# Attention scores from two float32r parts on half the array's rows in place of three bfloat16 parts

## The reference

```python
def _attn(q_in, k_in, v_in, wq, bq, wk, bk, wv, bv, wo, bo, causal):
    Q = (q_in @ wq + bq).reshape(Bq, Sq, H, HD)          # H, HD = 16, 16
    Kp = (k_in @ wk + bk).reshape(Bq, Sk, H, HD)
    V = (v_in @ wv + bv).reshape(Bq, Sk, H, HD)
    scores = jnp.einsum('bqhd,bkhd->bhqk', Q, Kp) / jnp.sqrt(jnp.float32(HD))
    if causal:
        scores = jnp.where(mask, scores, -jnp.inf)
    a = jax.nn.softmax(scores, axis=-1)
    o = jnp.einsum('bhqk,bkhd->bqhd', a, V).reshape(Bq, Sq, Dm)
    return o @ wo + bo
...
x = _layernorm(x + _attn(x, x, x, ..., True), ln1_g, ln1_b)
x = _layernorm(x + _attn(x, encoder_output, encoder_output, ..., False), ln2_g, ln2_b)
x = _layernorm(x + _moe(x, router_w, router_b, e_w1, e_b1, e_w2, e_b2), ln3_g, ln3_b)
```

## Time and profile before

| | |
|---|---|
| time, median of 3 runs | 755.05 us (754.03 to 757.26) |
| span of the profiled execution | 755.9 us |
| PE busy | 711.2 us, 94% |
| DVE busy | 499.0 us, 66% |
| ACT busy | 369.2 us, 49% |
| POOL busy | 287.3 us, 38% |
| mean DMA rate | 186 GB/s |

### The profile page before, as it was taken

One profiled execution on the slowest core, in us unless ns is written; L12 is line 12 of the kernel. 1 busy time (PEld: TensorE's weight loads), 2 busy tenths in 40 slices (PEclk: granted clock), 3 DMA queues, 4 the chain that ended last, 5 costly groups with the idle time before them and its releaser, 6 DMA issues.

```text
span 755.9 us, 14560 instructions
## 1 busy us (share of the span) xinstructions
PE 711.2 (94%) x4969; PEld 478.4 (63%) x4969; DVE 499.0 (66%) x1376; ACT 369.2 (49%) x749; POOL 287.3 (38%) x558
## 2 busy tenths in 40 slices
PE   6889999999999999999997889999999999999983
PEld 4444434545464454645563666898999999999941
DVE  5679788678766877756687744365666665666436
ACT  4325475665666676677753436433433332332403
POOL 8305521542653463624654333212332332232114
PEclk9999999999999999999997989999999999999997
DMA  8954431343164021316037762676999999999754
GB/s 273 291 145 128 114 98 46 84 129 128 34 179 127 13 60 48 92 43 179 14 113 237 223 210 95 204 262 226 357 328 343 343 326 341 343 332 333 236 187 163
DMA packets 95154, 140.29 MB, mean 186 GB/s; under 512 B 11855, under 2 KB 81077, under 8 KB 92597
## 3 DMA queue, kind: packets, MB, share of 16 engines
q1 hardware_dynamic: 76357, 107.86, 45.5%
q10 hardware_dynamic: 15072, 22.02, 9.1%
q0 software_dynamic: 3648, 9.45, 3.5%
HBM read 110.65 MB, written 28.65 MB: 184 GB/s over the span
## 4 chain that ended last, share of the span: by engine, by line
PE 75%; issue 8%; DVE 7%; DMA 5%; POOL 2%; ACT 1%; SPq 0%; DVEq 0%; ACTq 0%; POOLq 0%
PE out_acc L984 11%; PE score_pair L961 10%; PE work L932 9%; PE score_pair L855 8%; PE work L849 8%; PE work L906 6%; PE work L855 4%; PE score_pair L849 3%; PE work L1008 3%; DVE neg_part_max L1472 3%; PE work L918 2%; PE work L992 2%; PE work L935 2%; DMA arena<-parts_scratch 1%; PE out_acc L849 1%
## 5 line engine op out<-in xcount | busy, mean ns | idle before, releaser
L1472 DVE TENSOR_REDUCE neg_part_max<-work 128x1 f32<-128x512 f32 (+4 forms) x368 | 213.3, 625 | 70.4 <-PE work L935 35.9
L1244 ACT ACTIVATE arena<-score_pair 128x1024 f32<-128x1024 f32 (+2 forms) x224 | 178.9, 839 | 79.8 <-PE score_pair L961 78.9
L932 PE MATMUL work<-arena 96*128 96x77 bf16 (+4 forms) x640 | 118.5, 278 | 10.3 <-ACT arena L1207 2.7
L961 PE MATMUL score_pair<-arena 99*128 99x512 bf16 (+2 forms) x448 | 104.2, 337 | 4.0 <-DMA arena<-negmax_scratch 3.0
L984 PE MATMUL out_acc<-arena 128*32 128x512 f32 (+4 forms) x896 | 103.7, 517 | 2.6 <-DVE arena L1492 2.6
L1904 POOL DMA_INDIRECT chosen_scratch<-arena,scatter_rows x36 | 35.6, 989 | 176.5 <-DVE arena L1404 176.2
L855 PE MATMUL score_pair<-arena 128*128 128x256 f32 x432 | 97.6, 380 | 0.0
L932 PEld LDWEIGHTS work<-arena 96*128 96x128 bf16 x640 | 49.5, 99 | 74.5 <-issue 31.0
L1960 POOL TENSOR_SCALAR_AFFINE_SELECT arena<-arena 128x256 f32<-128x256 f32 x128 | 51.5, 410 | 117.9 <-ACT arena L1244 116.7
L1177 ACT ACTIVATE arena<-work,expert_b_cols 128x128 f32<-128x128 f32 x180 | 51.1, 369 | 77.3 <-PE work L849 64.0
L849 PE MATMUL work<-arena 128*128 128x128 f32 x720 | 87.7, 279 | 0.3 <-issue 0.3
(11 more groups left out here) (257 smaller groups left out, 955.0 us busy)
## 6 DMA issues: line engine op xcount, KB each, us to landing
arena<-in_L_xattn_e_w SPq DMA_DIRECT2D x54, 1024.0 KB, 7.1
arena<-parts_scratch SPq DMA_DIRECT2D x24, 768.0 KB, 6.1
arena<-in_L_xattn_e_w ACTq DMA_DIRECT2D x18, 1024.0 KB, 6.4
parts_scratch<-arena_more SPq DMA_DIRECT2D x24, 384.0 KB, 2.6
parts_scratch<-arena_more SPq DMA_DIRECT2D x24, 256.0 KB, 3.0
parts_scratch<-arena_more SPq DMA_DIRECT2D x24, 128.0 KB, 2.9
residual<-in_x SPq DMA_DIRECT2D x4, 512.0 KB, 8.1
tokens_scratch<-residual SPq DMA_DIRECT2D x2, 1024.0 KB, 5.4
```

The source lines that it names most:

```text
L932: m = pe.matmul(bank[:, j * it.w:(j + 1) * it.w], qa[st.half(it.g)][0:R_S, h, n0:n0 + P], k, start=True, stop=not it.last)
L961: m = pe.matmul(st2[pair][0:rows, j, 0:w], k, qa[st.half(it.g)][0:R_M, h, skip:QG], start=True, stop=True)
L1244: act_e.activation(pt[buf][0:rows, :, 0:w], st2[pair][0:rows, :, 0:w], ACT.Exp, scale=float(HD) ** -0.5).then_inc(pair_taken[pair], 1)
L1472: dve.tensor_reduce(pm[:, it.at, it.t, it.h0:it.h0 + it.nh], bank[:, 0:it.nh * it.w].rearrange("p (j k) -> p j k", j=it.nh), AX.X, ALU.max ...
```

## The change

Queries and keys are split into two float32r parts in place of three bfloat16 parts. float32r is float32 in memory; the first part is what is left when a float32 is written as float32r, the second the rest. There are then 3 groups (part pairings 0-0, 0-1, 1-0), so that a head takes 48 rows (`R_S`) and with two parts of the maximum 50 (`R_M`). Two heads, an even and an odd one, stand one above the other: in rows 0 to 49 and 64 to 113 (`ROWS` = 64). The key and query tiles hold `HALF` = 4 columns of heads of 4 bytes in place of 8 of 2 bytes.

A maximum's bank now holds heads of one half only (`pair`), and the pieces alternate between the halves. The mask is added from the same half, in two turns of 64 rows of the identity; the lower and the upper half of the mask are also kept exchanged in `mask_qk[:, 1]`, written by two small DMAs. A turn covers all heads of the bank. The cross keys are 78 wide (`SEW`), one column of it filler. The two matmuls of a score pair go to different halves, and each raises `pair_full`. `rest` becomes one subtraction on POOL, and for the stages in a hurry is gone from ACT and DVE. Maxima are split in two, transposed by one float32 matmul. ACT waits for `prob_taken` by name before it writes `pt`. The keys' and queries' tiles move to memory of their own, which the experts' weight rings use later. `ORDER` is new.

```diff
-Q_PART = (0, 0, 0, 1, 1, 2)
-K_PART = (0, 1, 2, 0, 1, 0)
+Q_PART = (0, 0, 1)
+K_PART = (0, 1, 0)
...
-R_M = R_S + 3
+R_M = R_S + 2
+ROWS = P // 2
+HALF = HH // 2
+SEW = SE + SE % 2
...
-            steps += [Item("max", st=st, t=qb, g=u, at=c, w=w, h0=h0, nh=BANK // w, last=(c + 1) * BANK >= keys)
-                      for h0 in range(0, HH, BANK // w)]
+            steps += [Item("max", st=st, t=qb, g=u, at=c, w=w, h0=h0, nh=BANK // w, last=(c + 1) * BANK >= keys, pair=j)
+                      for h0 in range(0, HALF, BANK // w) for j in range(2)]
...
-    "mwuqm2qmwm2q2m3wmgq2m3wqmqm2f2wmqfqm3wymqsfqm3wmf2wm2q2pm2qf2wuqm2vm2q2m2rf3wmq2lm2fwqm2f2wfqfqm3gqf2wqmdumf"
+    "wmq2dyfsumfwqm3qwm3fq2mwfqfmfmqmwqrmfdqrf2m2qmlwm2wqm3q2mwfm2wfqm2qmqpfmquwqm2vmqmwmqm2wmqmfqdmqwpfm2fqwmqgmfmufpf"
...
-                    for j in range(it.nh):
-                        h = it.h0 + j
-                        k = kac[st.slot][0:R_S, h, 0:it.w] if st.cross else ka[st.slot][0:R_S, it.at, h, 0:it.w]
-                        m = pe.matmul(bank[:, j * it.w:(j + 1) * it.w], qa[st.half(it.g)][0:R_S, h, n0:n0 + P], k,
-                                      start=True, stop=not it.last)
-                        if it.last:
-                            m = pe.matmul(bank[:, (j + 1) * it.w - P:(j + 1) * it.w], identb[:, :], mask_qk[:, :],
-                                          start=False, stop=True)
+                    half = it.pair * ROWS
+                    rows = slice(half, half + R_S)
+                    for i in range(it.nh):
+                        h = it.h0 + i
+                        k = kac[st.slot][rows, h, 0:it.w] if st.cross else ka[st.slot][rows, it.at, h, 0:it.w]
+                        m = pe.matmul(bank[:, i * it.w:(i + 1) * it.w], qa[st.half(it.g)][rows, h, n0:n0 + P].bitcast(f32r),
+                                      k.bitcast(f32r), start=(i == 0), stop=(i == it.nh - 1 and not it.last))
+                    rows = slice(half, half + ROWS)
+                    for turn in range(2 if it.last else 0):
+                        to = bank[:, 0:it.nh * it.w].rearrange("p (h k) -> p h k", h=it.nh)[:, :, it.w - P:it.w]
+                        mask = mask_qk[rows, turn, :].rearrange("p (o k) -> p o k", o=1)
+                        m = pe.matmul(to, identb[rows, turn * ROWS:turn * ROWS + P], bc(mask, [ROWS, it.nh, P]),
+                                      start=False, stop=(turn == 1))
...
-                    for t in range(QT):
-                        m = pe.transpose(rows[:, t * P:(t + 1) * P],
-                                         negp[:, it.g * QT + t, :, :].rearrange("p k h -> p (k h)"), identb[:, :])
-                    m.then_inc(full[it.bank], 1)
+                    pe.transpose(bank[0:2 * HH * QT, 0:P], negp[:, it.g].rearrange("p j k h t -> p (j k h t)"),
+                                 ident[:, :]).then_inc(full[it.bank], 1)
...
-                        h = it.quad * QUAD + it.pair * 2 + j
+                        h, part = it.quad * 2 + it.pair, slice(j * ROWS, j * ROWS + R_M)
...
-                        m = pe.matmul(st2[pair][0:rows, j, 0:w], k, qa[st.half(it.g)][0:R_M, h, skip:QG],
-                                      start=True, stop=True)
-                    m.then_inc(pair_full[pair], 1)
+                        m = pe.matmul(st2[pair][0:rows, j, 0:w], k.bitcast(f32r),
+                                      qa[st.half(it.g)][part, h, skip:QG].bitcast(f32r), start=True, stop=True)
+                        m.then_inc(pair_full[pair], 1)
...
-                    e.wait_ge(pair_full[pair], it.n // 2 + 1)
-
+                    e.wait_ge(pair_full[pair], 2 * (it.n // 2 + 1))
+
+                    e.wait_ge(prob_taken[buf], it.n // 4)
...
-                    own.inc(pool.tensor_tensor(f, f, p[0], ALU.subtract))
-                    e.wait_ge(gstep, own.n)
-                    own.inc(pool.tensor_copy(p[1], f))
-                    e.wait_ge(gstep, own.n)
-                    pool.tensor_tensor(p[2], f, p[1], ALU.subtract).then_inc(third_g, 1)
+                    pool.tensor_tensor(p[1], p[1], p[0], ALU.subtract).then_inc(second_g, 1)
...
-                        sp.dma_start(to.rearrange("p h t -> p (h t)"),
-                                     parts_d[st.n, at, it.g].rearrange("g (d h) t -> (g d) (h t)", h=HH)).then_inc(
-                            qk_in[st.half(it.g)], 16)
+                        for j in range(2):
+                            rows = slice(j * ROWS, j * ROWS + R_S)
+                            sp.dma_start(ka[st.slot][rows, it.g] if at else qa[st.half(it.g)][rows],
+                                         apart(parts_d[st.n, at, it.g], j)).then_inc(qk_in[st.half(it.g)], 16)
```

More of the change, by code:

```diff
@@ L39 @@
 R_S = NGR * HD
-R_M = R_S + 3
-TWO_ONES = float(np.array([0x3F803F80], np.uint32).view(np.float32)[0])
+R_M = R_S + 2
+ROWS = P // 2
+HALF = HH // 2
+SEW = SE + SE % 2
 NEG = -1e30
@@ L168, in maxima @@
         if st.cross:
-            steps += [Item("max", st=st, t=qb, g=u, w=SE, h0=h0, nh=HH // 2) for h0 in range(0, HH, HH // 2)]
+            steps += [Item("max", st=st, t=qb, g=u, w=SEW, nh=HALF, pair=j) for j in range(2)]
             continue
@@ L373, in build @@
 def build(nc, x, ctx_in, par, wts, router_w, w1, b1, w2, b2, out):
[L374 removed]
+    f32, f32r, bf16, i32, u32 = (mybir.dt.float32, mybir.dt.float32r, mybir.dt.bfloat16, mybir.dt.int32,
+                                 mybir.dt.uint32)
     ALU, ACT, AX = mybir.AluOpType, mybir.ActivationFunctionType, mybir.AxisListType
@@ L460, in build @@
         b1_rows = onat_words[1][0:E * FC, D:D + P]
-        part_words = cut("more", 3 * S)
-        part_sb = [part_words[:, a * 3 * S // 2:(a + 1) * 3 * S // 2].bitcast(bf16).rearrange("p (k t) -> p k t", k=3)
-                   for a in range(2)]
-        mT = cut_bf("more", QG)
+        part_words = cut("more", 4 * S)
+        part_sb = [part_words[:, a * 2 * S:(a + 1) * 2 * S].rearrange("p (k t) -> p k t", k=2) for a in range(2)]
+        mT = cut("more", P)
         rT = [cut("more", D).rearrange("p (c n) -> p c n", c=KC) for _ in range(2)]
@@ L546, in build @@
         n_used = sb("tiles_used", [1, 1], i32)
+        with nc.sbuf_tensor("keys_queries", [P, KEYS], f32) as keys_t:
+            keys = keys_t[:, :]
+            ka = [keys[:, a * HALF * S:(a + 1) * HALF * S].rearrange("p (u h t) -> p u h t", u=NG, h=HALF) for a in range(2)]
+            k0 = 2 * HALF * S
+            qa = [keys[:, k0 + a * HALF * QG:k0 + (a + 1) * HALF * QG].rearrange("p (h t) -> p h t", h=HALF)
+                  for a in range(2 * NG)]
+            k0 += 2 * NG * HALF * QG
+            kac_words = keys[:, k0:KEYS]
+            kac = [kac_words[:, a * HALF * 80:(a + 1) * HALF * 80].rearrange("p (h t) -> p h t", h=HALF) for a in range(2)]
+        late = sb("weights_results", [P, KEYS])
+        w1_ring = [late[:, a * EW:(a + 1) * EW].rearrange("p (c f) -> p c f", c=KC) for a in range(RING1)]
+        w2_ring.insert(0, late[:, RING1 * EW:(RING1 + 1) * EW].rearrange("p (c n) -> p c n", c=FC))
+        assert (RING1 + 1) * EW <= 2 * HALF * S and len(w2_ring) == RING2
+        chosen = late[:, 2 * HALF * S:2 * HALF * S + 2 * NT * D].rearrange("p (c t n) -> p c t n", c=2, t=NT)
         st2 = [stack.enter_context(nc.psum_tensor(f"score_pair{i}", [P, 2, BANK], f32)) for i in range(2)]
```

186 lines of the change are left out of this document (83 added, 103 removed).

## The result

The changed kernel takes 832.09 us (median of 4 runs, 830.09 to 852.29), the kernel before 754.99 us beside it: ratio 1.1005, 95% interval 1.0966 to 1.1045. One of the four executions (852.29 us) is a slow one, which ratios leave out, and where the profiled execution of an experiment was such a one (e5, e6, e7, e13), the others' clock is given beside it. The profiled execution spans 828.5 us, 72.6 more than before. The forecast of 741 us was wrong, in its direction too, and the time lies 7 us above the range.

A forecast was written before the change was run, and what follows sets the result against it. TensorE (PE) was taken to bound attention, so PE work was summed: scores -38.1, maxima -18, masks +13.9, loads +19, shape changes +12.5, transposes -1.8, start -2, giving -14.5 from 755: 741 us, range 716 to 825.

The forecast's parts named there:

- Price of a column, 0.42 ns: Score matmuls: a float32r column was taken to stream in 0.42 ns, as in bf16; bounds 0.42 and 1.69.
- Halves side by side: Scores: the two heads of a pair run together in lower and upper rows, 76.3 us becoming 38.2, saving 38.1.
- Loads, +19: Weight loads on PE that come into the open, at the transposes' 0.06 us each, add 19 us; ends +2 and +46.
- slow loads: Rival: float32r weight loads cost 0.11 us, as float32's; +27 on the sum, 768 us, chance 0.22.
- Changes of shape, +12.5: PE switching between half and whole array: 156 more switches at 0.08 us add 12.5 us; ends zero and 23.
- The sum of PE's work, -14.5: All terms, mostly PE work in attention, together were to take 14.5 us off the kernel's 755.
- two cycles: Rival: a float32r column in scores and maxima takes 0.84 ns; +67 in all, 822 us, chance 0.20.
- A microsecond of PE work there is nearly a microsecond of the kernel: Attention stretch, 60 to 400 us: PE runs with hardly a gap, so the forecast is a sum of PE work.
- The stretch's DMA share of 0.31 covers that: Attention stretch: SP's twice as many loads, moving the same bytes, were to cost nothing, DMA share being 0.31.
- The start, -2: First maximum, at 26.99 us before: shorter chain but four loads for two, -2 us net; ends 0 and -4.
- ACT's wait for pt: ACT's wait by prob_taken before exponentials, for which PE waits: 0 us; 13 if it bound once per block.
- No relief from DVE: Rival: PE gets lighter but DVE's 368 reductions and their three banks set the pace; 754 us, chance 0.05.

The follow-up runs named there:

- e5: Changed kernel with spare bf16 matmuls at five places where PE waits for keys or queries: 826.35 us, ratio 1.0886.
- e6: Changed kernel with scores and maxima reading the upper two bytes of each float32r value as bf16: 814.69 us, ratio 1.0736.
- e7: Changed kernel with both matmuls of every score pair on rows 0 to 49, so they can't run side by side: 895.16 us, ratio 1.1805.
- e13: Changed kernel with the old order, the two maxima of a pair neighbours and their matmuls issued by turns: 827.17 us, ratio 1.0901.
- e10: Kernel before with maxima and scores on rows 0 to 47 and masks on rows 0 to 63: 799.53 us, ratio 1.0536.
- e12: Changed kernel with the old order, maxima and scores reading all 64 rows of their half: 798.21 us, ratio 1.0531.
- e14: Changed kernel with the old order, paired maxima issued by turns, and 64 rows a half in scores and maxima: 812.04 us, ratio 1.0731.
- e11: Changed kernel, new order, with maxima and scores reading all 64 rows of their half in place of 48 and 50: 837.62 us.
- e9: Kernel before with maxima and scores on rows 0 to 47, masks still on all 128 rows: 909.09 us, ratio 1.1935.
- e2: Changed kernel with the order string of the kernel before: 813.03 us, ratio 1.0772.
- e4: Kernel before with each load of keys or queries cut into two DMAs of 2 KB pieces: 759.29 us, ratio 1.0054.

## Why the prediction was wrong

Some pieces of the changed kernel's chain at full clock, maxima, masks, scores:

```profile
152.26 0.38 PE score_pair L980 x2
152.65 0.17 PE work L950
152.82 0.13 PE work L956 x2
...
154.81 0.26 PE score_pair L980 x2
155.06 0.22 PE work L950
155.29 0.13 PE work L956 x2
155.42 0.12 PE score_pair L980 x2
155.53 0.31 PE work L950
155.84 0.32 PE score_pair L980 x2
156.16 1.91 PE work L922 x4
```

- **Price of a column, 0.42 ns: right.** No row of before shows this term of the sum for float32r; it was my estimate, the lowest of the bounds from the earlier trace rows. What the changed kernel shows in its place: a pair of 512 columns costs 0.32 (155.84), its load of 0.11 included, which leaves 0.41 ns a column. At 0.84 ns its stream alone would be 0.43.
- **Halves side by side: right.** The same row: two streams and two loads in 0.32, where one after the other they would be 0.43 before any load. In the timeline the two of a pair start 3 ns apart.
- **Loads, +19: too small in the unit.** They cost 0.11, not 0.06, and could not be hidden at 78 and 128 columns (0.57 for four of 78; two of 128 in a row usually start 0.11 apart at full clock, in e6 0.06). That was the rival 'slow loads', and its mechanism is true; e6 gives the size, some 20 us.
- **Changes of shape, +12.5: about right.** 0.10 each where I had 0.08; e10's 143 cost 13 us by the account.
- **Maxima beside their neighbours, -18:** not measured by itself.
- **The sum of PE's work, -14.5: the account says -2, the cruder one +4.** With slow loads it would have been +12.5, so the rest came out 8 to 14 better than I had it. So far nothing that would make 832. The rival 'two cycles' had 805 to 870 us, and 832 lies in it by coincidence alone: its column of 0.84 ns is refuted by the pair's 0.32.
- **"A microsecond of PE work there is nearly a microsecond of the kernel": the step that failed.** It held the clock constant and had no term for it. The earlier trace rows shows 1.00 in both stretches, and I read it as a property of the chip and not as something that the kernel before earns. What I named as making all of it wrong (a price by width, a dearer change of shape) did not come; the clock stood nowhere in the prediction. The half-row layout that made scores side by side leaves a lone maximum with 48 rows. By the account the clock costs 45 us. That fewer rows can do this is shown in the kernel before (e10, 42 us, with 143 more changes of shape as the rest of the difference) and for the score pairs (e7). In the changed kernel 64 rows in place of 48 to 50 give back 13 to 18 us (e12, e14), while e11 did not show it; filling five waits takes 25 to 55 us off its half clock (e5), and changes of shape have a part (e9 against e10). How the 45 divide among the three was not measured.
- **"The stretch's DMA share of 0.31 covers that": wrong.** The share is 0.35 in the same stretch after, hardly more, and yet PE waits 15.1 us for keys and queries in place of 2.2. One of them, in the chain:

```profile
91.16 10.83 DMA keys_queries<-parts_scratch
```

  The order of before has 10.0 (e2), so 5 of these are the new order's; e4 gives cut loads some 4 us of time at most.
- **The start, -2: wrong.** The chain's wait for the first keys, against the earlier trace rows, and SP's loads in the timeline:

```profile
26.34 6.37 issue
```

```profile
20.05 3.26 SPq L2093 DMA_DIRECT2D keys_queries<-parts_scratch  x4
```

  The first maximum starts at 32.70 us in place of 28.38. The loads are issued no earlier (20.05 against 19.67) and land later.
- **The order** had no term of its own; it costs 18 us (e2).
- **ACT's wait for pt**: PE waits 3.0 us for ACT's exponentials in the attention in place of 1.0. Zero was nearly right.
- **No relief from DVE**: it is not the bound after, as 1.3 us of waiting show; it becomes one when maxima are paired (15.2 us, e13).

## What to carry to other kernels

When a change makes matmuls use fewer rows of the array, put a term for the clock into the sum (42 us in e10): look at the granted clock of the stretch, and at what was at work while it was full. Before a theory of the clock is dropped, look at the mean clock of every execution and not at the profiled one alone: here it ranged from 72 to 120 us at half clock in one program (e5). In e13 cheaper matmuls (30 us less work than e2) saved no time, since the banks were not free (15.2 us of waiting), so price the wait that is next late (loads' landing, free banks), not the bandwidth. An order tuned for one set of durations is a change of its own (18 us here, e2); try the new code with the old order first.

## What was not expected of the hardware

- A PE busy throughout can be at half clock: 50 us at 0.50 with 48 rows in use, 1.00 with 96 (e10). Later the same 48 rows have 1.00 for 290 us. Even 48 to 64 rows of a half is worth 13 to 18 us (e12, e14; not in e11).
- More changes of shape go with more half clock: 274 us with 838 of them, 114 with 391, both on 48 rows (e9, e10).
- A microsecond at half clock costs 0.4 to 0.5 us: 42 us for 86 more (e10), 45 for 97 (after), 22 for 53 between two executions of the changed kernel.
- Going from a half of the rows to all of them, or back, costs 0.10 us (e9's masks at 0.16 in place of 0.06).
- float32r streams a column in 0.41 ns (a pair of 512 in 0.32 us less a load of 0.11), as bf16 does (0.42), but its weights take 0.11 us to load; reading the same memory as bf16 with a stride brings four 78-column maxima from 0.57 to 0.25 us.
- In both halves not only the streams but also the loads run side by side, 3 to 4 ns apart.
- A load of 384 KB on 48 rows lands in 7.2 us, on 96 rows in 5.1, both in 2 KB pieces. Why is open.
